# Two attention layers of a transformer stack: the output projection of a token tile moves one step later

## The reference, cut to what matters

```python
# layer 2: keys and values from context and latents together, 4 key/value heads
hidden_states = concatenate([context, latents], axis=1)          # 128 keys per batch
q = latents @ Wq ; k = hidden_states @ Wk ; v = hidden_states @ Wv
attn = softmax(einsum('bhgqd,bkhd->bhgqk', q, k) / sqrt(128))
x = x + tanh(g_xattn[2]) * (einsum('bhgqk,bkhd->bqhgd', attn, v) @ Wo)

# layer 3: rotary positions, causal mask, 8 key/value heads, 64 keys per batch
queries = rope(q @ Wq.T) ; keys = rope(k @ Wk.T) ; values = v @ Wv.T
attn = softmax(where(causal, queries keys^T / sqrt(128), min))
x = x + tanh(g_xattn[3]) * ((attn @ values) @ Wd.T)
```

## Time and profile before

| | before |
|---|---|
| median of 3 runs | 1805.06 us |
| the profiled execution, its own time | 1810.68 us |
| its span, first to last instruction | 1808.9 us |
| PE busy (matmul) | 1594.0 us, 88% of the span |
| DVE, ACT, POOL busy | 952.2, 698.4, 628.2 us |
| mean granted TensorE clock | 0.948 |

### The profile page before, as it was taken

The page is one execution under the profiler, slowest core; times in us unless marked ns, Lnnn a source line. Parts: engine busy times, 40 slices in busy tenths (PEclk is TensorE's granted clock), DMA queues, the critical chain, the costliest instruction groups (busy, mean ns, idle before and its releaser), DMA issues. The chain is left out here.

```text
span 1808.9 us, 29350 instructions
## 1 busy us (share of the span) xinstructions
PE 1594.0 (88%) x10450; PEld 1330.0 (74%) x10450; DVE 952.2 (53%) x1857; ACT 698.4 (39%) x2015; POOL 628.2 (35%) x594
## 2 busy tenths in 40 slices
PE   5887879859699999999999996968999999999976
PEld 4655666548588988888888895757778877877853
DVE  4885668777424322331432326686565656655653
ACT  3443154344335435443452533442333234224221
POOL 2542244475313212321331321334343534434410
PEclk9997999969899999999999999879999999999986
DMA  5001110021301100110000001231112112211001
GB/s 193 1 1 47 40 37 1 1 85 52 85 27 48 36 24 25 44 39 19 30 24 24 25 24 54 98 88 59 59 35 74 54 35 81 70 54 39 13 3 47
DMA packets 27865, 81.14 MB, mean 45 GB/s; under 512 B 3248, under 2 KB 11952, under 8 KB 22768
## 3 DMA queue, kind: packets, MB, share of 16 engines
q1 hardware_dynamic: 26896, 79.44, 13.2%
q10 hardware_dynamic: 864, 0.30, 0.1%
HBM read 69.25 MB, written 10.49 MB: 44 GB/s over the span
## 5 line engine op out<-in xcount | busy, mean ns | idle before, releaser
L386 PE MATMUL bank<-hid_high,wq_high 128*128 128x256 f32 x1152 | 343.6, 298 | 6.5 <-DVE probs_last L1181 5.8
L386 PE MATMUL bank<-hid_low,wq_high 128*128 128x256 f32 x1152 | 327.1, 284 | 0.0
L386 PE MATMUL bank<-hid_high,wq_low 128*128 128x256 f32 x1152 | 327.0, 284 | 0.0
L386 PE MATMUL bank<-wo_high,out_high 128*128 128x512 f32 x576 | 241.5, 419 | 43.5 <-DVE out_low L1231 37.6
L1239 DVE SCALAR_TENSOR_TENSOR x_stream<-bank,gates,x_stream 128x512 f32<-128x512 f32 x128 | 96.1, 751 | 266.6 <-PE bank L386 266.6
L386 PEld LDWEIGHTS bank<-hid_high,wq_high 128*128 128x128 f32 x1152 | 221.9, 193 | 14.4 <-issue 10.1
L386 PE MATMUL bank<-wo_low,out_high 128*128 128x512 f32 x576 | 230.8, 401 | 0.0
L386 PE MATMUL bank<-wo_high,out_low 128*128 128x512 f32 x576 | 229.8, 399 | 0.0
L1025 POOL TENSOR_TENSOR probs_middle<-probs_middle,small 128x512 f32<-128x512 f32 x64 | 66.7, 1042 | 458.4 <-DVE small L1226 458.4
L386 PEld LDWEIGHTS bank<-hid_low,wq_high 128*128 128x128 f32 x1152 | 222.3, 193 | 2.9 <-issue 2.9
L386 PEld LDWEIGHTS bank<-hid_high,wq_low 128*128 128x128 f32 x1152 | 221.8, 193 | 0.0
(11 more groups left out here) (255 smaller groups left out, 3504.2 us busy)
## 6 DMA issues: line engine op xcount, KB each, us to landing
raw_q<-in_L_wq SPq DMA_DIRECT2D x18, 1024.0 KB, 5.1
raw_o<-in_L_wo SPq DMA_DIRECT2D x18, 1024.0 KB, 4.9
values_last<-ctx_values SPq DMA_DIRECT2D x32, 256.0 KB, 3.9
values_t_last<-ctx_keys SPq DMA_DIRECT2D x8, 512.0 KB, 5.3
raw_c<-in_L_wkv SPq DMA_DIRECT2D x6, 512.0 KB, 5.3
x_stream<-in_x SPq DMA_DIRECT2D x8, 256.0 KB, 9.8
ctx_keys<-raw_o SPq DMA_DIRECT2D x8, 256.0 KB, 2.0
ctx_values<-raw_o SPq DMA_DIRECT2D x16, 128.0 KB, 2.4
```

What stands on the lines that cost most here:

```text
L386: last = k.nc.tensor.matmul(out, stationary(a, c), moving(b, c), start=n == 0, stop=n == total - 1)
```

## The change

Projection and update of tile t stand in step t + 4 of a unit instead of t + 3. Every unit has 12 steps on every engine (before: 11, and 12 where a unit of layer 2 carries the next keys and values). The layer norm statistics in the last unit move along, and the next unit's queries stay in steps 8 to 10.

```diff
     LAG = 2
+    LAG_Y = LAG + 2
...
-    SLOTS = T + LAG + (1 if rope else 2)
+    SLOTS = T + LAG_Y
...
-                    for t in range(SLOTS if ahead else T + LAG + 1):        # ScalarE, VectorE, TensorE
+                    for t in range(SLOTS):
...
-                        if t >= T and not rope and u < UN - 1:              # ScalarE
+                        if T <= t < T + AHEAD and not rope and u < UN - 1:
                             queries(j, u + 1, t - T)
...
-                        if LAG + 1 <= t <= T + LAG:                         # VectorE
-                            update(t - LAG - 1)
-                        tile = t - LAG - 2
+                        if LAG_Y <= t:
+                            update(t - LAG_Y)
+                        tile = t - LAG_Y - 1
...
-                        if t >= T and u < UN - 1:                           # TensorE
+                        if T <= t < T + AHEAD and u < UN - 1:
...
-                            if i == 0 and t == LAG + 1:
+                            if i == 0 and t == LAG_Y:
                                 pe.wait_ge(k.lo_o, v("lo_o", j, 4 * UN, 4 * u + 4))
-                            if i == 0 and LAG + 1 <= t <= T + LAG:
-                                project(t - LAG - 1)
+                            if i == 0 and LAG_Y <= t:
+                                project(t - LAG_Y)
                         if LAG <= t < T + LAG:
                             attend(t - LAG)
```

More of the change, by code:

```diff
@@ L1247, in body @@
                     ahead = u == UN - 1 and not last
-                    for t in range(SLOTS if ahead else T + LAG + 1):
+                    for t in range(SLOTS):
                         if t < T:
```

## The result

The changed kernel takes 1833.26 us (median of 4 runs, 1831.55 to 1835.12) against 1805.69 us of the kernel before (median of 4): a ratio of 1.0153, 95% interval 1.0136 to 1.0171. It is slower by 27.6 us. The forecast was 1805.5 us with a range of 1794 to 1816, so the time lies outside it, and the kernel lost where a draw was expected.

The account below looks back on a forecast made before the run. TensorE, busy 88%, was taken as the bound through its standstills. From the profiled 1810.68 us, 33.0 removed and 32.4 added gave 1810.1, or 1804.5 against the median; 1 us added made 1805.5, range 1794 to 1816.

Parts of the forecast that it names:

- Removed waits: TensorE, both layers: all 48 projection waits on `out_low` go, 33.0 us won for good.
- the 2.63 carried over: Layer 3, seven units: 2.63 us standing still at step 7's end remains, moving mostly to the next queries' wait on `wq_low`.
- Step 3: Every unit: `attend(1)` directly follows its transposes, adding 1.65 us in layer 2 and 0.79 in layer 3, 19.5 in sum.
- Step 11: `project(6)` and `project(7)` back to back on one PSUM bank; the second waits for `update(6)`, 0.99 us 13 times, 12.9 us.
- Layer 2: Sum of the forecast's gains and added waits in layer 2: 7.4 us slower.
- What is late next at the end of step 7: Layer 3: step 6 projection's end to next `queries` stays 7.74 us on VectorE and POOL; nothing won there in seven units.
- The clock: Lowered TensorE clock: 1.5 us per layer 3 unit more or less; 1 us added to the forecast.
- rival D: Paired step 2 and 3 gaps in layer 2 lower the clock, 1.5 us each: 15 us slower, 1819.5 us; chance 0.16.
- B: Layer 3's step 7 chain doesn't hold, low halves are in time: 18 us and clock falls go, 1780 us; chance 0.10.
- C: Waits go and nothing is paid, steps 3 and 11 being hidden: 1760 us; chance 0.03.

Follow-up runs that it names:

- after_early: Changed kernel with layer 3's split of the next query weights made in step 4 instead of 5 and 6: 1786.2 us, 0.9893 of the kernel before.
- early_cover: after_early with, in both layers, the transposes of a step put ahead of its queries: 1746.71 us, ratio 0.9672 to the kernel before.
- before_collide: Kernel before plus two spare POOL subtractions in step 5 of layer 3, putting the weight split on the keys' rotation: 1826.75 us, ratio 1.0113.
- early_spare: after_early plus spare POOL subtractions in layer 3 where the weight split was (steps 5 and 6): 1791.36 us, ratio 0.9917 to the kernel before.

## Why the prediction was wrong, point by point

- **Removed waits** (33.0 us): right. The 48 waits of projections on `out_low` went. In after_early, where nothing is carried over, a looped unit of layer 3 takes 61.4 us; the forecast's 63.7 less the 2.63 carried over is 61.1.
- **Step 3** (19.5 us): right. The waits on L1404 doubled from 11.2 to 22.9 us, those on L1398 from 4.2 to 8.5, and early_cover with all of them gone met what was expected of it within 1 us.
- **Step 11** (0.99 us, 13 times): right in place and number, a little large in size. 15 waits on `x_stream` appear, 13 of them of 0.84 to 1.03 us, 11.8 us in sum against 12.9.
- **Layer 2** (7.4 us slower): right, 8.8 measured.
- **What is late next at the end of step 7**: this step failed. It saw the right chain and the right place, but took "7.74 us, on VectorE and POOL alone" as fixed. It measured 10.31 us. The rotation takes 3.8 us instead of 2.1, since it now lies on POOL's split, and the split behind it 3.38 instead of 2.53. This is 2.57 us in seven units, 18 us, and no rival had it. With 1.8 us for the clock under the queries it makes the forecast unit of 63.7 us the measured one of 68.1. The argument compared which instruction waits for which, and not what now runs at the same time: the removed wait had also been the distance between the two engines.
- **The clock**: forecast as 1 us, with rival D looking for falls in layer 2. Layer 2 has one, as before, so D fell. In layer 3 the falls come at the end of step 7, in 7 of 7 units, and the queries pay 1.5 to 1.95 us for each, where before five cost about 1.4. About 5 us.
- Rivals B and C fell: the chain holds, and the prices of steps 3 and 11 are paid.

Against the profiled execution the account closes, by sizes read from the changed kernel itself. It grew by 22.4 us (1810.68 to 1833.08): start of layer 3 6.4 us later, its looped units 22.0 us longer, the end from the last unit on 6.0 us shorter. The forecast's -0.6, with the 18 and the 5 added, is 22. The medians differ by 27.6, as the profiled run of the kernel before was 5 us above its median; that difference isn't explained by anything here.

The Trainium skill has the rule that was missed ("SBUF — State Buffer", section "SBUF: two separate sides"): VectorE and GpSimd share one pair of SBUF ports, and of an operation of VectorE with two SBUF inputs and one of GpSimd that reads SBUF, whichever starts first holds the pair for its whole instruction while the other is blocked. The trace agrees in the order. In step 6 the first POOL subtraction starts ahead of the rotation (1412.38 against 1412.74), keeps its 1.27 us, and the rotation operation grows to 1.46. In step 7 the rotation starts ahead of the split (1418.84), keeps its 0.68, and the subtraction beside it takes 1.71; from there on their ends alternate (POOL 1420.55, VectorE 1421.11, POOL 1422.22):

```profile
1418.75 0.68 DVE L1180 TENSOR_TENSOR probs_t_last<-values_t_last,rope 128x512 f32<-128x512 f32 x1
1419.45 1.66 DVE L1181 TENSOR_TENSOR probs_last<-values_t_last,rope 64x512 f32<-64x512 f32 x1
```

It agrees less in the size: a pair takes 1.66 to 1.71 us where 0.69 and 1.27 add up to 1.96, so some 0.3 us of the two still overlap. And `out_low`, which reads one operand from PSUM, stays at 0.69 us in every version, also beside a POOL operation of 1.29 us (1416.63 in the unit above). That the shared ports are the reason is the skill's account; the runs show the stretch, the order and which operations have it.

## What to carry to other kernels

A wait also keeps work apart. Before taking one away, lay the lists of VectorE and GpSimd side by side at their new times and look for operations whose operands all lie in SBUF on both; the duration in a row holds only beside the neighbours that it had there. When every wait on a chain is accounted and the forecast is a draw between gains and new waits, the new waits are the next edits: here three small moves turned a loss of 1.5% into a gain of 4.0%.

## What the runs showed of the hardware

- A VectorE operation of 0.69 us with both inputs in SBUF takes up to 1.70 us beside POOL subtractions, and these grow from 1.27 to up to 1.75 us each. Where two meet first, the one that started first keeps its time. One operation of VectorE and one of POOL alternate, so a longer POOL list stretches more of them: 2.05 us for the three of a rotation without POOL, 2.94 to 3.07 with one stretched, 3.83 to 4.06 with two.
- The granted clock fell to the 1.2 GHz level at a standstill of 2.38 us in five of seven units of the kernel before, and at one of 4.0 us (bracket) in seven of seven of before_collide. In the changed kernel it fell in all seven, where three standstills of 0.95, 0.84 and 2.90 us (brackets of the unit shown) follow each other with only `attend` and two transposes between them; it fell at 1419.56 in the unit shown, 0.2 us into the third, and in the first looped unit 0.8 us ahead of it, so the long one alone is not what lowered it. It never fell behind the 1.65 us standstills of layer 2, though two of them stood 6.6 us apart. With no standstill over 0.9 us in the units of layer 3 (after_early, early_spare) the mean over all seven is 1.00.
